# Storing rotated query and key rows as (row, head), and fetching their stacks in four transfers a quad instead of ten

## The chip, the cores and the metric

The kernel runs on one core of one Trainium2 chip. The metric is the device time of one execution in microseconds (us), smaller is better. The kernel before took 1014.62 us (median of 3 runs, 1014.4 to 1017.1).

## The reference

Two transformer-like layers run over an input `x` of 8 batches, 512 positions and 256 channels, float32:

```
xn = layernorm(x)
x  = x + attention(xn) + int8_ffn(xn)                  # layer 0
xn = layernorm(x)
x  = x + gated_comparison(xn) + receptance_ffn(xn)     # layer 1
```

Only the attention of layer 0 matters here. It has 16 heads of 64 channels:

```
q = (x @ Wq + bq).reshape(b, s, 16, 64);  k likewise;  v likewise
q, k = rope(q), rope(k)        # x0*cos - x1*sin , x0*sin + x1*cos, halves concatenated
scores = q @ k.T / 8, causal;  attn = softmax(scores);  out = (attn @ v) @ Wo + bo
```

The even channels of a head (32 of them) rotate against its odd channels (32).

## The kernel before, in words

Every float32 matrix product is split into float16 high and low parts (`wh`, `wl` for weights, `xsh`, `xsl` for the columns of x, which the page calls by these names). All of layer 0 runs in a ring of turns: `ring(n)` on each engine handles pair n of heads, 64 pairs in all (8 batches of 8 pairs), and starts at n = -5 with turns that only prepare. Four heads, two pairs, are a quad; there are 32 quads.

Queries and keys of a quad are made in two phases, f = 2*quad for the queries and f = 2*quad + 1 for the keys. A phase goes like this:

- PE, `quad_block` (L1717, matmuls at L1713): even channels of four heads into one bank, odd channels into another; 128 rows each, four heads of 32 rows.
- DVE, `even_terms` and `odd_terms` (L1378, L1392): bias from `bcol` added, multiplied with the tables `cosq`, `sinq` or `cosk`, `sink`: four products of 128x512.
- POOL, `rotate` (L616): difference and sum, `r_e` and `r_o`. ACT, `high_e` and `high_o` (L888, L896): float16 copies `hi_e`, `hi_o`. POOL, `low_e` and `low_o` (L627, L635): the remainders `lo_e`, `lo_o`.
- SP, `move_queries` or `move_keys` (L492, L506): each of these four tiles of 128x512 float16 (128 KB) is stored to DRAM (`scr`) when it is made, and read back rearranged so that the 64 channels of one head lie on the partitions: `qs` holds for each head 32 rows high even, 32 high odd, 32 low even, 32 low odd. `kd` holds the key's high parts twice (rows 0 to 63 and 64 to 127), `kz` its low parts in rows 0 to 63 and zeros under them.

`scores` (L1772) multiplies `qs` with `kd` and then with `kz` (matmuls at L1784 and L1785). The stacks exist twice, by quad parity. The first scores of a quad wait for all its loads; the loads wait for the scores of the quad before the last (`s_done`), and each load waits for the store whose data it reads (`hie_sent` and so on).

Before the change, row 32*h + r of such a tile is row r of head h. A load must therefore pick, for each of 32 partitions, four pieces of 1 KB that lie 32 KB apart in `scr`. There are four loads for a query stack and six for a key stack, 128 KB each.

What orders the work: each engine has its own list of instructions in program order, written out by hand in its `ring`, and semaphores between them. SP's list has, quad by quad, the query stores and loads, now and then stores and loads of the columns of x, then the key stores and loads. All transfers of the kernel are issued from SP.

The row order is set in three places that run once. `halves` (L396) names the source and target columns in which ACT (`act.activation`, L848, eight instructions) and DVE (`pairs_low`, L1250, instructions at L1256, sixteen) write the weights of q and k into `wh` and `wl`. The load at L463 (sixteen small transfers) lays the biases in `bcol`. `rotation_tables` (L2088) builds the tables on the host. In the preparing turns the DVE runs `pairs_low(G_Q)`, the first four rotation products, `pairs_low(G_K)`, four more products, then the weight maxima (L1215) and row statistics (L1156, L1160), and so on; ACT runs the eight weight copies and then `row_sums` (L819 to L833) of five batches.

Of the kernel before, what the change touches and what calls it, by code (L numbers as in the profile page):

```python
# [9 lines left out]
L = 64  # L10
P = 128
# [18 lines left out]
HL = L // 2  # L30
C_QK = 0
# [12 lines left out]
def build(nc, x_d, weights_d, w8_d, bqk_d, vec_d, thr_d, gate_d, tab_d, out_d):  # L44
# [11 lines left out]
    with ctx:  # L56
# [339 lines left out]
        def halves(g):  # L396

            a = g - G_Q
            for e in range(2):
                for pp in range(2):  # L400
                    src = wst_qk.rearrange("p (kq x) -> p kq x", x=8 * L)[:, :, pp * 4 * L:(pp + 1) * 4 * L]
                    src = src.rearrange("p kq (c i) -> p kq c i", i=L)[:, :, PAIR[g], e * HL:(e + 1) * HL]
                    at = (2 * a + e) * P + pp * L
                    yield src, [w[:, C_QK:C_V].rearrange("p (kq x) -> p kq x", x=8 * L)[:, :, at:at + L]
                                .rearrange("p kq (s i) -> p kq s i", s=2) for w in (wh, wl)]

        def wgroup(w, g):

# [38 lines left out]
        def _(sp):  # L447
# [12 lines left out]
            for h in range(4):  # L460
                for a, c in ((0, 1 + h % 2), (1, 3 * (h % 2))):
                    for e in range(2):
                        sp.dma_start(bcol[h * HL:(h + 1) * HL, :, a, e], b4[:, :, h // 2, c, e],  # L463
                                     allow_slow_non_contiguous=True).then_inc(b_loaded, 16)
            load_rows(3)
            load_rows(4)
# [16 lines left out]
            def fetch_columns(b):  # L483
# [5 lines left out]
                for c in range(2):  # L489
                    sp.dma_start(xs[u][c][:], xscr[b, c]).then_inc(x_in[u], 16)  # L490

            def move_queries(quad, par):  # L492

                f = 2 * quad
                after(sp, q_in[par], 64 * (quad // 2))
                for piece, tile, made_by, sent in ((0, hi_e, hie_done, hie_sent), (1, hi_o, hio_done, hio_sent),
                                                   (2, lo_e, loe_done, loe_sent), (3, lo_o, loo_done, loo_sent)):
                    sp.wait_ge(made_by, f + 1)
                    sp.dma_start(scr[par, 0, piece], tile).then_inc(sent, 16)
                after(sp, s_done, 12 * (quad - 1))  # L500
                for piece, sent in enumerate((hie_sent, hio_sent, loe_sent, loo_sent)):
                    sp.wait_ge(sent, 16 * (f + 1))
                    sp.dma_start(qs[par][piece * HL:(piece + 1) * HL],
                                 scr[par, 0, piece].rearrange("(h r) s -> r h s", h=4)).then_inc(q_in[par], 16)

            def move_keys(quad, par):  # L506

                f = 2 * quad + 1
                after(sp, k_in[par], 96 * (quad // 2))
                for piece, tile, made_by, sent in ((0, hi_e, hie_done, hie_sent), (1, hi_o, hio_done, hio_sent),  # L510
                                                   (2, lo_e, loe_done, loe_sent), (3, lo_o, loo_done, loo_sent)):
                    sp.wait_ge(made_by, f + 1)
                    sp.dma_start(scr[par, 1, piece], tile).then_inc(sent, 16)
                after(sp, s_done, 12 * (quad - 1))
                sp.wait_ge(kz_zero, 2)
                for piece, sent in enumerate((hie_sent, hio_sent, loe_sent, loo_sent)):
                    sp.wait_ge(sent, 16 * (f + 1))
                    rows = scr[par, 1, piece].rearrange("(h r) s -> r h s", h=4)
                    at = (piece % 2) * HL
                    if piece < 2:  # L520
                        sp.dma_start(kd[par][at:at + HL], rows).then_inc(k_in[par], 16)
                        sp.dma_start(kd[par][L + at:L + at + HL], rows).then_inc(k_in[par], 16)
                    else:
                        sp.dma_start(kz[par][at:at + HL], rows).then_inc(k_in[par], 16)

            def send_maxima(turn, src, count):

# [1133 lines left out]
        def _(pe):  # L1661
# [110 lines left out]
            def scores(n, h, tiles):  # L1772

                if absent(n):
                    return
                g = 2 * n + h
                par, hh = n // 2 % 2, n % 2 * 2 + h
                if h == 0 and tiles[0] == 1 and hh == 0:
                    pe.wait_ge(q_in[par], 64 * (n // 4 + 1))
                    pe.wait_ge(k_in[par], 96 * (n // 4 + 1))  # L1780
                after(pe, max_done, 4 * g - 4 + {1: 1, 0: 3, 3: 4}[tiles[0]])
                for i in tiles:
                    out, q = s_tile[i], qs[par][:, hh, i * P:(i + 1) * P]
                    pe.matmul(out, q, kd[par][:, hh, 0:(i + 1) * P], start=True, stop=False)  # L1784
                    last = pe.matmul(out, q, kz[par][:, hh, 0:(i + 1) * P], start=False, stop=True)  # L1785
                last.then_inc(s_done, 1)
# [301 lines left out]
def rotation_tables():  # L2088
# [3 lines left out]
    freq = (np.float32(1.0) / np.float32(10000.0) ** (np.float32(2.0) * np.arange(half, dtype=np.float32) / np.float32(L)))  # L2092
    ang = (np.arange(SQ, dtype=np.float32)[:, None] * freq.astype(np.float32)[None, :]).astype(np.float32)
    t = np.stack([np.cos(ang.astype(np.float64)).T, np.sin(ang.astype(np.float64)).T], axis=1).astype(np.float32)
    return np.ascontiguousarray(np.tile(t, (4, 1, 1)))


# [37 lines left out]
```

## Time and profile before

| | |
|---|---|
| median of 3 runs | 1014.62 us |
| the profiled execution, its own time | 1014.82 us |
| its span (first to last instruction) | 1012.3 us |
| PE busy | 973.6 us, 96% of the span |
| DVE / POOL / ACT busy | 840.8 / 776.1 / 744.4 us |
| packets on the one queue that carries data | 102784, 99.81 MB, 32.6% of 16 DMA engines' time |
| granted TensorE clock | 0.999 of full speed |

The span is what the trace covers; the 2.5 us between it and the execution's own time lie around it. PE busy counts overlapping matmuls once, so short waits between them can hide in it. A number such as L1784 is a line of the kernel.

### The profile page before, as it was taken

What the parts mean: (1) busy time and instruction counts of PE and PEld (TensorE: products, weight loads), DVE (VectorE), ACT (ScalarE), POOL (GpSimd) and SP (SyncE); (2) the same over time, 40 slices, a digit from 0 to 9 for tenths busy, and PEclk for the clock granted to TensorE, in tenths of its full rate; (3) what the DMA queues carried; (4) which work ended last, traced back from release to release, by engine and by line L of the source; (5) the groups of instructions that cost most, each with busy time, mean ns of one, the idle gap of its engine ahead of it and who ended that gap; (6) DMA issues with size and microseconds to landing.
All of it is one profiled execution on the core that took longest, in us unless ns stands there. A gap on an engine that the chain in (4) does not pass through costs nothing.

```text
span 1012.3 us, 23657 instructions
## 1 busy us (share of the span) xinstructions
PE 973.6 (96%) x7956; PEld 673.0 (66%) x7956; DVE 840.8 (83%) x2259; ACT 744.4 (74%) x1998; POOL 776.1 (77%) x959
## 2 busy tenths in 40 slices
PE   5889999999999999999999999999999999899998
PEld 4556665766666666666666666666666676677776
DVE  7989999788879888877787878877788778989995
ACT  5989987666676677766767676766666776889994
POOL 3777768778777787878787878787877565899995
PEclk9999999999999999999999999999999999999999
DMA  8733445243442333233333333433333200111111
GB/s 261 254 111 118 151 129 153 82 131 106 124 118 86 107 119 95 88 106 111 95 96 115 95 95 96 119 100 102 98 95 96 73 2 16 34 47 35 49 55 43
DMA packets 102902, 101.31 MB, mean 100 GB/s; under 512 B 13952, under 2 KB 98560, under 8 KB 102144
## 3 DMA queue, kind: packets, MB, share of 16 engines
q1 hardware_dynamic: 102784, 99.81, 32.6%
q8 instruction: 65, 1.06, 0.5%
q14 instruction: 53, 0.43, 0.2%
HBM read 56.25 MB, written 40.90 MB: 96 GB/s over the span
## 4 chain that ended last, share of the span: by engine, by line
PE 75%; DVE 10%; POOL 6%; ACT 4%; issue 2%; DMA 2%; SPq 0%; DVEq 0%; POOLq 0%; ACTq 0%
PE bank L1713 24%; PE bank L1810 13%; PE bank L1796 12%; PE bank L1827 8%; PE bank L1784 6%; PE bank L1785 5%; PE bank L2014 3%; PE bank L1954 3%; DVE arena L1410 2%; POOL arena L651 2%; DVE arena L1426 2%; POOL arena L714 2%; ACT arena L919 1%; DMA arena<-in_weights 1%; DVE arena L1388 1%
## 5 line engine op out<-in xcount | busy, mean ns | idle before, releaser
L651 POOL TENSOR_SCALAR arena<-arena,rc 128x128 f32<-128x128 f32 (+3 forms) x512 | 278.2, 562 | 176.5 <-DVE rc L1419 175.5
L919 ACT ACTIVATE arena<-arena,nm 128x256 f32<-128x256 f32 (+3 forms) x512 | 283.4, 554 | 109.0 <-DVE nm L1410 104.3
L1410 DVE CUSTOM_DVE_ANT_0 arena<-bank,mask_rows 128x256 f32<-128x256 f32 (+3 forms) x512 | 232.9, 483 | 88.6 <-PE bank L1785 83.4
L1796 PE MATMUL bank<-ident,arena 128*128 128x128 f32 x1280 | 211.8, 278 | 9.7 <-DVE arena L1426 4.4
L1796 PEld LDWEIGHTS bank<-ident,arena 128*128 128x128 f32 x1280 | 150.0, 141 | 68.6 <-DVE arena L1426 29.2
L1785 PE MATMUL bank<-arena 128*128 128x256 f16 (+3 forms) x512 | 152.9, 299 | 0.0
L1810 PE MATMUL bank<-arena 128*64 128x512 f32 (+3 forms) x1024 | 152.0, 439 | 0.0
L1784 PE MATMUL bank<-arena 128*128 128x256 f16 (+3 forms) x512 | 139.9, 300 | 1.5 <-DMA arena<-scr 1.5
L1810 PEld LDWEIGHTS bank<-arena 128*64 128x64 f32 x1024 | 67.8, 136 | 95.0 <-issue 70.6
L1426 DVE COPY arena<-bank 128x512 f32<-128x512 f32 (+3 forms) x256 | 124.6, 487 | 3.3 <-PE bank L1796 2.9
L927 ACT ACTIVATE arena<-bank 128x512 f32<-128x512 f32 (+3 forms) x256 | 108.6, 424 | 14.9 <-PE bank L1796 14.2
L1713 PE MATMUL bank<-xsh,wh 128*128 128x512 f16 x256 | 97.1, 379 | 3.2 <-DVE wl L1256 2.4
L1827 PE MATMUL bank<-wh,arena 128*128 128x256 f16 x512 | 99.7, 273 | 0.0
L1713 PE MATMUL bank<-xsh,wl 128*128 128x512 f16 x256 | 97.0, 379 | 0.0
L1713 PE MATMUL bank<-xsl,wh 128*128 128x512 f16 x256 | 97.0, 379 | 0.0
L919 ACT ACTIVATION_READ_ACCUMULATOR arena<-arena,nm 128x1 f32 x512 | 96.0, 187 | 0.0
L937 ACT ACTIVATE arena<-bank,bvs 128x512 f16<-128x512 f32 x64 | 44.0, 687 | 69.7 <-PE bank L1810 69.4
L1713 PE MATMUL bank<-wh,xsh 128*128 128x128 f16 x512 | 89.1, 219 | 1.9 <-DVE arena L1401 1.9
L1713 PE MATMUL bank<-wh,xsl 128*128 128x128 f16 x512 | 89.1, 219 | 0.0
L1713 PE MATMUL bank<-wl,xsh 128*128 128x128 f16 x512 | 89.1, 219 | 0.0
L623 POOL TENSOR_TENSOR arena<-arena 128x512 f32<-128x512 f32 x64 | 81.6, 1275 | 5.5 <-DVE arena L1401 5.4
L625 POOL TENSOR_TENSOR arena<-arena 128x512 f32<-128x512 f32 x64 | 83.0, 1296 | 0.0
(192 smaller groups left out, 2176.2 us busy)
## 6 DMA issues: line engine op xcount, KB each, us to landing
arena<-scr SPq DMA_DIRECT2D x320, 128.0 KB, 2.7
scr<-arena SPq DMA_DIRECT2D x256, 128.0 KB, 1.7
arena<-in_weights SPq DMA_DIRECT2D x5, 1024.0 KB, 7.8
x_sb<-in_x SPq DMA_DIRECT2D x8, 512.0 KB, 9.4
out<-x_sb SPq DMA_DIRECT2D x16, 256.0 KB, 2.2
xscr<-arena SPq DMA_DIRECT2D x12, 256.0 KB, 3.2
arena<-wh SPq DMA_DIRECT2D x40, 64.0 KB, 2.0
xsh<-xscr SPq DMA_DIRECT2D x6, 256.0 KB, 3.4
```

The costliest lines, as they stand in the source:

```text
L625: pool.tensor_tensor(r_o, t_es, t_oc, ALU.add).then_inc(r1_done, 1)
L651: last = pool.tensor_scalar(pr[slot][:, OFF[i]:OFF[i + 1]], pr[slot][:, OFF[i]:OFF[i + 1]], rc[:, slot, i:i + 1], 1.0, ALU.mult, ALU.mult)
L919: act.activation(pr[slot][:, OFF[i]:OFF[i + 1]], pr[slot][:, OFF[i]:OFF[i + 1]], ACT.Exp, scale=-1.0, bias=nm[:, slot, i:i + 1], accum_out ...
L927: act.activation(ptf[h][:, TOFF[j]:TOFF[j + 1]], (pt0, pt1)[h][:, 0:P * (NT - j)], ACT.Copy).then_inc(ptf_done[h], 1)
L1410: dve.tensor_tensor_reduce(pr[slot][:, OFF[i]:OFF[i + 1]], s_tile[i], mask_rows[:, SQ - P * (i + 1):SQ], -1.0, -MASKED, ALU.add, ALU.min, ...
L1426: dve.tensor_copy(ptf[1][:, TOFF[j]:TOFF[j + 1]], pt1[:, 0:P * (NT - j)]).then_inc(ptf_done[1], 1)
L1713: last = pe.matmul(out, lhs, rhs, start=(a == 0), stop=(a == len(pairs) - 1))
L1784: pe.matmul(out, q, kd[par][:, hh, 0:(i + 1) * P], start=True, stop=False)
L1785: last = pe.matmul(out, q, kz[par][:, hh, 0:(i + 1) * P], start=False, stop=True)
L1796: last = pe.transpose(banks[5 + h][:, (i - j) * P:(i - j + 1) * P], pr[2 * par + h][:, OFF[i] + j * P:OFF[i] + (j + 1) * P], ident[:])
L1810: last = pe.matmul(ob[h * L:(h + 1) * L, j * P:SQ], vf[:, j, h * L:(h + 1) * L], ptf[h][:, TOFF[j]:TOFF[j + 1]], start=(j == 0), stop=(j = ...
L1827: last = pe.matmul(bank[:, t * D:(t + 1) * D], o[:, slot, rows], w[:, p, :], start=(p == 0 and a == 0 and t == 0), stop=(p == NP - 1 and a ...
```

## The change

Row 4*r + h of the four tiles is now row r of head h. The weights, the biases and the tables are laid out for that order. In `scr` the four heads of one row then lie side by side, 4 KB, and pieces follow each other, so the query stack is one contiguous read of 512 KB into 128 partitions; the key stack takes three reads of 256 KB into 64 partitions each. Stores are the same. The query load now waits for all four stores; both loads of `kd` wait for both high stores, the load of `kz` for both low stores. The wait for `kz_zero` moves behind the loads of `kd`. The counts on `q_in` and `k_in` follow (64 to 16, 96 to 48).

```diff
 def halves(g):
-                    at = (2 * a + e) * P + pp * L
-                    yield src, [w[:, C_QK:C_V].rearrange("p (kq x) -> p kq x", x=8 * L)[:, :, at:at + L]
-                                .rearrange("p kq (s i) -> p kq s i", s=2) for w in (wh, wl)]
+                    at = (2 * a + e) * P
+                    yield src, [w[:, C_QK:C_V].rearrange("p (kq x) -> p kq x", x=8 * L)[:, :, at:at + P]
+                                .rearrange("p kq (i n s) -> p kq n s i", n=2, s=2)[:, :, pp] for w in (wh, wl)]
...
-                        sp.dma_start(bcol[h * HL:(h + 1) * HL, :, a, e], b4[:, :, h // 2, c, e],
+                        sp.dma_start(bcol[h:P:4, :, a, e], b4[:, :, h // 2, c, e],
...
+            def stacked(pieces):
+                return pieces.rearrange("c (r h) s -> (c r) h s", h=4)
...
 def move_queries(quad, par):
...
                 after(sp, s_done, 12 * (quad - 1))
-                for piece, sent in enumerate((hie_sent, hio_sent, loe_sent, loo_sent)):
+                for sent in (hie_sent, hio_sent, loe_sent, loo_sent):
                     sp.wait_ge(sent, 16 * (f + 1))
-                    sp.dma_start(qs[par][piece * HL:(piece + 1) * HL],
-                                 scr[par, 0, piece].rearrange("(h r) s -> r h s", h=4)).then_inc(q_in[par], 16)
+                sp.dma_start(qs[par], stacked(scr[par, 0])).then_inc(q_in[par], 16)
 def move_keys(quad, par):
...
                 after(sp, s_done, 12 * (quad - 1))
+                for sent in (hie_sent, hio_sent):
+                    sp.wait_ge(sent, 16 * (f + 1))
+                for rows in (slice(0, L), slice(L, P)):
+                    sp.dma_start(kd[par][rows], stacked(scr[par, 1, 0:2])).then_inc(k_in[par], 16)
                 sp.wait_ge(kz_zero, 2)
-                for piece, sent in enumerate((hie_sent, hio_sent, loe_sent, loo_sent)):
+                for sent in (loe_sent, loo_sent):
                     sp.wait_ge(sent, 16 * (f + 1))
-                    rows = scr[par, 1, piece].rearrange("(h r) s -> r h s", h=4)
-                    at = (piece % 2) * HL
-                    if piece < 2:
-                        sp.dma_start(kd[par][at:at + HL], rows).then_inc(k_in[par], 16)
-                        sp.dma_start(kd[par][L + at:L + at + HL], rows).then_inc(k_in[par], 16)
-                    else:
-                        sp.dma_start(kz[par][at:at + HL], rows).then_inc(k_in[par], 16)
+                sp.dma_start(kz[par][0:L], stacked(scr[par, 1, 2:4])).then_inc(k_in[par], 16)
...
 def rotation_tables():
-    return np.ascontiguousarray(np.tile(t, (4, 1, 1)))
+    return np.ascontiguousarray(np.repeat(t, 4, axis=0))
```

The target columns of the weights follow from it: in `wh` and `wl` the 32 values of one head were neighbours (2 bytes apart) and are now every fourth (8 bytes apart). The DVE reads `wh` and writes `wl` in that order too.

## Rows read from the trace of the kernel before

**Rows 1.** The page's part 4, the chain that ended last, shares by engine
```profile
PE 75%; DVE 10%; POOL 6%; ACT 4%; issue 2%; DMA 2%; SPq 0%; DVEq 0%; POOLq 0%; ACTq 0%
```
**Rows 2.** Busy time by stretch: us, PE, PEld, DVE, ACT, POOL, clock, DMA share, GB/s
```profile
63.00:200.00 137.00, 133.00 (x1049) 85.31 (x1049) 122.71 (x341) 113.14 (x309) 102.98 (x134) 1.00 0.41 123
200.00:800.00 600.00, 597.24 (x4920) 407.80 (x4919) 487.50 (x1434) 416.38 (x1172) 468.74 (x608) 1.00 0.35 105
```
**Rows 3.** Waits of PE: us in total, times, longest; the only one for a stack
```profile
PE bank L1784 <- DMA arena<-scr: 1.5, 1, 1.5
```
**Rows 4.** The chain of waits from 17 to 48 us: start, us, what
```profile
18.07 1.67 DVE wl L1256 x3
...
20.40 2.07 DVE wl L1256 x5
...
25.44 1.61 DVE wl L1256 x2
...
27.16 1.89 DVE wl L1256 x2
...
39.61 0.67 DVE arena L1401
...
47.75 0.49 ACT arena L919
```
**Rows 5.** SP's and PE's timelines in mid-ring: start, us, what
```profile
415.27 1.75 SPq L503 DMA_DIRECT2D arena<-scr  x4
423.66 3.08 SPq L513 DMA_DIRECT2D scr<-arena  x4
426.85 0.36 SPq L521 DMA_DIRECT2D arena<-scr  x1
...
428.71 0.90 SPq L524 DMA_DIRECT2D arena<-scr  x2
...
431.53 0.28 PE L1784 MATMUL bank<-arena 128*128 128x256 f16 x1
...
443.73 0.28 PE L1784 MATMUL bank<-arena 128*128 128x256 f16 x1
```
**Rows 6.** The page's part 6, DMA issues: count, KB each, median us to landing
```profile
arena<-scr SPq DMA_DIRECT2D x320, 128.0 KB, 2.7
scr<-arena SPq DMA_DIRECT2D x256, 128.0 KB, 1.7
...
xsh<-xscr SPq DMA_DIRECT2D x6, 256.0 KB, 3.4
```
**Rows 7.** SP's timeline around the first stacks
```profile
36.98 2.23 SPq L513 DMA_DIRECT2D scr<-arena  x4
...
41.15 0.30 SPq L521 DMA_DIRECT2D arena<-scr  x1
...
41.98 0.90 SPq L524 DMA_DIRECT2D arena<-scr  x2
```
**Rows 8.** Timelines of ACT, PE, DVE at the first scores; idle before in brackets
```profile
41.70 0.63 ACT L894 ACTIVATE arena<-arena 128x512 f16<-128x512 f32 x1 [0.40 <-POOL arena L623]
...
45.36 0.27 PE L1784 MATMUL bank<-arena 128*128 128x256 f16 x1 [1.48 <-DMA arena<-scr]
...
47.87 2.35 DVE L1247 SCALAR_TENSOR_TENSOR wl<-arena,inv,wh 128x2048 f16<-128x2048 f32 x1 [0.23 <-ACT wh L837]
```
**Rows 9.** Groups of instructions by shape: busy us, mean ns
```profile
L1229 DVE TENSOR_REDUCE wall<-wl 128x5 f32<-128x640 f32 x1 | 1.3, 1344 | 0.0
L1215 DVE TENSOR_REDUCE wmax<-arena 128x1 f32<-128x2048 f32 x1 | 2.3, 2276 | 0.0
L1215 DVE TENSOR_REDUCE wmax<-arena 128x1 f32<-128x512 f32 x3 | 2.0, 676 | 0.0
L874 ACT ACTIVATE w<-arena 128x512 bf16<-128x512 int32 x1 | 0.7, 652 | 0.0
L902 ACT ACTIVATE arena<-arena 128x512 f16<-128x512 f32 x64 | 39.3, 614 | 0.6 <-POOL arena L625 0.6
```

More of the change, by code:

```diff
@@ L490, in fetch_columns @@
                     sp.dma_start(xs[u][c][:], xscr[b, c]).then_inc(x_in[u], 16)
+            def stacked(pieces):
+                return pieces.rearrange("c (r h) s -> (c r) h s", h=4)
             def move_queries(quad, par):
                 f = 2 * quad
-                after(sp, q_in[par], 64 * (quad // 2))
+                after(sp, q_in[par], 16 * (quad // 2))
                 for piece, tile, made_by, sent in ((0, hi_e, hie_done, hie_sent), (1, hi_o, hio_done, hio_sent),
@@ L500, in move_queries @@
                 after(sp, s_done, 12 * (quad - 1))
-                for piece, sent in enumerate((hie_sent, hio_sent, loe_sent, loo_sent)):
+                for sent in (hie_sent, hio_sent, loe_sent, loo_sent):
                     sp.wait_ge(sent, 16 * (f + 1))
-                    sp.dma_start(qs[par][piece * HL:(piece + 1) * HL],
-                                 scr[par, 0, piece].rearrange("(h r) s -> r h s", h=4)).then_inc(q_in[par], 16)
+                sp.dma_start(qs[par], stacked(scr[par, 0])).then_inc(q_in[par], 16)
             def move_keys(quad, par):
                 f = 2 * quad + 1
-                after(sp, k_in[par], 96 * (quad // 2))
+                after(sp, k_in[par], 48 * (quad // 2))
                 for piece, tile, made_by, sent in ((0, hi_e, hie_done, hie_sent), (1, hi_o, hio_done, hio_sent),
@@ L1778, in scores @@
                 if h == 0 and tiles[0] == 1 and hh == 0:
-                    pe.wait_ge(q_in[par], 64 * (n // 4 + 1))
-                    pe.wait_ge(k_in[par], 96 * (n // 4 + 1))
+                    pe.wait_ge(q_in[par], 16 * (n // 4 + 1))
+                    pe.wait_ge(k_in[par], 48 * (n // 4 + 1))
                 after(pe, max_done, 4 * g - 4 + {1: 1, 0: 3, 3: 4}[tiles[0]])
```

## The prediction

> **What bounds the kernel now.** I read the chain of waits first. PE carries 75% of it, DVE, POOL and ACT 20% together, DMA 2% and SP's queue 0% [rows 1]. The busy times by stretch then say where PE is not full: from 200 to 800 us it is busy 597.2 of 600, from 63 to 200 us 133.0 of 137 [rows 2], so the ring is bound by PE and the whole idle time there that anything could give back is 6.8 us. Last the waits of PE: of 32 quads exactly one, the first, makes PE wait for a stack, for 1.5 us [rows 3]. The transfers that the change rebuilds are therefore hidden in 31 of 32 quads. What is left is the front: from 17 to 48 us the chain runs over DVE, where the weights' low parts (L1256) stand on it with 12 of their 16 instructions (the other four run beside PE and end just as it needs them), then over POOL and ACT [rows 4]. That is where the new row order writes with gaps.
>
> **The change, part by part.**
>
> *Ring: loads of the stacks.* Removed are 3 query and 3 key issues a quad; SP spends 1.75 us on four query loads and 426.85 to 429.61, 2.76 us, on six key loads [rows 5], about 0.44 and 0.46 an issue, so some 2.7 us of SP's time a quad go. SP is on the chain with 0% and spends its time waiting for tiles to be made; worth 0. What could hurt is that a large load lands later than four small ones, and that the query load waits for the last store. Cover: in mid-ring the query loads of a quad start at 415.27 and its key loads at 426.85, the last key issue ends at 429.61; its first score is at 443.73 [rows 5] (one turn of the ring is 443.73 - 431.53 = 12.2 us, the quad's query loads stand in turn 2 x quad - 4 and its first score in turn 2 x quad - 1). So the last key load has 14.1 us from the end of its issue, and needs about 3. A load of 128 KB lands in 2.7 us, one of 256 KB in 3.4 [rows 6]: 0.7 more for 128 KB more. A 512 KB load would then take 3.4 + 2 x 0.7 = 4.8 us and a key load 3.4, or some 4.8 for the third in a row. Cover gone would need landings of over 14 us. Cost of this part 0 in 31 quads, and I expect 0 gain too, for the same reason: nothing that PE waits for becomes earlier. Fewer and larger packets (320 loads of 128 pieces of 1 KB become 10240 pieces of 4 KB) shorten DMA time that nobody waits for.
>
> A load that starts earlier can't collide with much either: the stores are unchanged, and a query load's 512 KB are off the DMA engines long before the key stores 8.4 us later (415.27 to 423.66 [rows 5]).
>
> *First quad.* Here the key stack is late by 1.5 us as PE sees it. Before, the four key stores are issued from 36.98 to 39.21, the second one's data is only in place at 41.15, and the last load is issued by 42.88 [rows 7]; PE starts at 45.36, 2.5 us after that [rows 8]. After, the same stores come first. SP has one query issue instead of four, so the first key store can go some 0.4 us earlier (it starts at 36.98, the moment the last query issue ends), the last one can't, for it waits for POOL. Both high loads then go at 40.8 to 41.15, the low one 0.9 us later, between 41.7 and 42.4. With 3.4 us for 256 KB that is 45.1 to 45.8, and 0.4 more if it queues behind the other two: the stack lands between 45.1 and 46.2, against 45.36, so -0.3 to +0.8, most likely +0.2. What is it worth? If earlier: nothing. The chain passes over ACT (its row sums and the copy of the next weights, L919 at 47.75 [rows 4]) and not over these scores. If later: DVE must finish the four maxima of these scores before L1247, which waits 0.23 us for ACT anyway [rows 8]; so the first 0.23 us or so are free and the rest is on the path. Bounds 0 to +0.6, taken +0.1. Where the 1.5 us go: PE's next idle time is for DVE and POOL, which the same chain sets.
>
> *Weights, DVE.* Sixteen instructions of 256 elements now read `wh` and write `wl` 8 bytes apart, all on the chain. No such DVE row is in the trace, so bounds. From above: the reduction L1229 reads 640 elements 20 bytes apart in 1344 ns; packed, L1215 shows (2276 - 676)/1536 = 1.04 ns an element, so 640 packed would be 676 + 128 x 1.04 = 809, and the gaps cost 535 ns, 0.84 an element [rows 9]. 16 x 256 x 0.84 = 3.4 us. From below 0: packed elements already pass at about one per cycle in this instruction and can't become faster by gaps. The nearest row is ACT's L874, which reads int32 exactly 8 bytes apart: 652 ns against 614 for the packed copy of the same size, L902 [rows 9], that is 0.04 us for 512 elements. By that 4096 elements cost 0.3 us. I take +0.2.
>
> The Trainium skill, "SBUF — State Buffer", section "Door 1: The DMA port swizzle", says that SBUF serves lines of 16 bytes and that accesses run at full rate as long as two fall in each line. By that rule 8 bytes apart is free and 20 bytes apart is not, and the sum would have 0 here; both trace rows agree with it in kind (0.04 us, 535 ns).
>
> *Weights, ACT.* Eight copies of 512 elements with gapped writes: by L874 8 x 0.04 = 0.3 us, by the upper slope 8 x 512 x 0.84 = 3.4 us, beside the DVE ones, not on top: DVE follows ACT half by half. ACT's next wait is 0.40 us at 41.70 [rows 8], so up to 0.4 us is absorbed there, but until then its high tiles are late and with them the first stack (cover 0.23 as above). Taken +0.
>
> *Biases and tables.* Sixteen transfers of 0.5 KB to partitions 4 apart instead of 32 neighbours, the same number of pieces; the tables come whole from the host. Before, the sum over the biases starts without a wait. 0, bounds -0.1 to +0.5, from nothing better than that SP's issue of the small ones already takes longer than that of a large one.
>
> *Moved wait and merged waits.* The key loads of the first quad wait for their stores and not for POOL's zeros, which precede its first rotation; 0. The query load's wait for the last store keeps SP from nothing: behind it are the stores of the next phase, whose tiles are not yet made.
>
> Once more a rule that speaks against the change. The Trainium skill, same page and section, says that 64 partitions reach no more of the memory's ports than 32 and gives 196 GB/s for 64 of them. By that figure 256 KB pass in an estimated 1.3 us, and two of the three key loads share one half, which puts the last of them at about 45.5 in the first quad and nowhere near 14 us in the ring; no row here shows a load to 64 partitions. It would change the sum by less than 0.1 us.
>
> **Sum.** Ring 0, first stack +0.1, weights +0.2, rest 0: +0.3 us on a profiled execution of 1014.82 (span 1012.3 and 2.5 around it), which lies 0.2 above the median of the runs. On the median: 1014.62 + 0.3 = 1014.9 us.
>
> A difference below 0.3%, 3.0 us, can't be told from none here.
>
> **Rivals.**
>
> A, slower: *gapped writes are dear.* DVE pays the slope of L1229 on its sixteen weight instructions, and nearly all of them stand on the chain [rows 4]: +3.4 us, and ACT's delay adds up to 0.6 over the first stack: 1018.3 to 1018.9. It decides from 0.7 ns an element (3.0 us over 4096). For it: L1229 shows that gaps can cost. Against: there each element has its own line, at 20 bytes, and L874 at 8 bytes shows a tenth of that. Chance 0.11.
>
> B, a little faster: *the first stack does matter.* The 1.5 us wait goes in part and the front moves with it, since the chain that I read picks one releaser of several: 1014.6 - 1.5 = 1013.1. Against: the chain runs through ACT with no wait for these scores before 47.75 [rows 4]. Within 0.3%. Chance 0.15.
>
> C, faster: *the loads disturb the engines.* If engines run slower beside 1 KB pieces than beside 4 KB ones, the idle time of PE in the ring goes: at most 6.8 us, 1007.8; half of it 1011.2. For it: PE loses 4.0 us in 63 to 200 us, where DMA is at 0.41, and 2.8 in 600 us at 0.35 [rows 2]. Against: the chain in the first stretch is long on extra DVE work, none of it on a DMA. Chance 0.09.
>
> D, *it doesn't do what it says:* the single large read is spread over few DMA engines. At the mean rate in the profile, 99.81 MB in 32.6% of 16 x 1012.3 us, one engine moves 18.9 GB/s, and 768 KB on one would take 42 us, 27 too late in every quad: hundreds of us. The stores, equally contiguous in DRAM, land in 1.7 us [rows 6], so no. Chance 0.02.
>
> **How the numbers follow.** My case, no measurable change, has 0.63; with B 0.78, the chance of within 0.3%. Faster by more is C, 0.09; slower by more is A and D, 0.13. The range takes my case with both ends (0 to +3.4 for weights, 0 to +0.6 for the stack), B, and half of C: 1012.0 to 1018.3.
>
> **What would show it.** Loads of `arena<-scr` x128, with 32 of 512 KB landing in 4 to 5.5 us and 96 of 256 KB in 3 to 4.5. L1256 at 470 to 500 ns, L848 at 707 to 750. PE's wait at L1784 once, 1 to 2.3 us, L1401 of the third phase within 0.3 us of 39.61, PE busy 597 of 600 between 200 and 800. I am wrong if L1256 takes over 640 ns, if a second wait of L1784 for a DMA shows up, or if the ring between 200 and 800 moves by more than 2 us while PE's work is the same.

## The result

The kernel after takes 1021.37 us (median of 6 runs, 1018.85 to 1022.43), the kernel before in the same comparison 1014.78 us (1014.28 to 1017.1): a ratio of 1.0055, 95% interval 1.0044 to 1.0067. The medians differ by 6.6 us, and by the ratio the kernel is slower by 5.6 us (4.5 to 6.8), more in either case than the 3 us that count as a difference. The prediction was 1014.9 us, "no measurable change", with a range of 1012.0 to 1018.3. It was wrong, and the time lies above every rival but the broken transfer, D.

### The profile page after: what moved, and what is told of

The parts are those of the page before. It is cut to its first block, busy times and chain, and to the rows that moved or that the text cites. A ratio compares the mean times of both kernels' runs of the same rounds, so it can differ in the third digit from the quotient of the medians.

```text
span 1019.2 us, 23531 instructions
## 1 busy us (share of the span) xinstructions
PE 978.2 (96%) x7956; PEld 674.0 (66%) x7956; DVE 844.9 (83%) x2259; ACT 748.8 (73%) x1998; POOL 776.5 (76%) x959
## 4 chain that ended last, share of the span: by engine, by line
PE 75%; DVE 10%; ACT 5%; POOL 4%; DMA 3%; issue 2%; SPq 1%; DVEq 0%; POOLq 0%; ACTq 0%
PE bank L1714 24%; PE bank L1811 13%; PE bank L1797 12%; PE bank L1828 8%; PE bank L1785 6%; PE bank L1786 5%; PE bank L2015 3%; PE bank L1955 3%; DVE arena L1411 2%; POOL arena L652 2%; DVE arena L1427 2%; DMA scr<-arena 1%; POOL arena L715 1%; DMA arena<-in_weights 1%; ACT wh L849 1%
## 5 line engine op out<-in xcount | busy, mean ns | idle before, releaser
L1785 PE MATMUL bank<-arena 128*128 128x256 f16 (+3 forms) x512 | 140.2, 301 | 3.5 <-DMA arena<-scr 3.5
L938 ACT ACTIVATE arena<-bank,bvs 128x512 f16<-128x512 f32 x64 | 44.0, 687 | 70.2 <-PE bank L1811 70.0
```

## The profile after

The profiled execution took 1021.75 us, with a span of 1019.2 us (before 1012.3). Line numbers outside SP's list are one higher than before: L849 is L848, L1257 is L1256, L1785 is L1784. From the page: the shares of the chain by engine, then three lines of part 6 (count, KB each, median us to landing).

```profile
PE 75%; DVE 10%; ACT 5%; POOL 4%; DMA 3%; issue 2%; SPq 1%; DVEq 0%; POOLq 0%; ACTq 0%
...
scr<-arena SPq DMA_DIRECT2D x256, 128.0 KB, 1.8
arena<-scr SPq DMA_DIRECT2D x96, 256.0 KB, 4.2
arena<-scr SPq DMA_DIRECT2D x32, 512.0 KB, 3.2
```

Against [rows 1] SP's queue and the DMAs have come onto the chain. Whether the ring or the front lost is read with a marker that exists once a turn: ACT's first copy of a turn's output (L937, after L938). Timeline of ACT in the kernel before, turns 0 and 63 (start, us, what):

```profile
67.89 0.69 ACT L937 ACTIVATE arena<-bank,bvs 128x512 f16<-128x512 f32 x1 [0.46 <-PE bank L1810]
...
843.04 0.69 ACT L937 ACTIVATE arena<-bank,bvs 128x512 f16<-128x512 f32 x1 [1.72 <-PE bank L1810]
```

The same of after:

```profile
74.14 0.69 ACT L938 ACTIVATE arena<-bank,bvs 128x512 f16<-128x512 f32 x1 [0.47 <-PE bank L1811]
...
849.25 0.69 ACT L938 ACTIVATE arena<-bank,bvs 128x512 f16<-128x512 f32 x1 [1.72 <-PE bank L1811]
```

Turn 0 is late by 6.25 us, turn 63 by 6.21. In between the ring lost nothing; this difference is made ahead of turn 0. The 0.7 us that the span shows beyond it lie behind turn 63's marker, from which the traces run for another 169.3 us before and 170.0 after; the work there is the same. Busy times by stretch of after, the second stretch set 6.2 us later so that it covers the same turns (columns as in [rows 2]):

```profile
206.20:806.20 600.00, 597.26 (x4920) 407.80 (x4919) 487.40 (x1434) 416.24 (x1172) 468.70 (x608) 1.00 0.35 105
```

That is [rows 2] again. The new landing times (4.2 and 3.2 us) are in the ring, and PE doesn't notice them. Its waits, after (us in total, times, longest):

```profile
PE bank L1714 <- DVE wl L1257: 4.1, 2, 2.6
PE bank L1785 <- DMA arena<-scr: 3.5, 1, 3.5
```

Still one wait for a stack in 32 quads, but 3.5 us in place of the 1.5 of [rows 3]. The chain of the front in after, from the weight copies to the first scores (start, us, what; left out between are mainly the row sums of three batches and the query's high copies):

```profile
16.73 9.48 ACT wh L849 x8
...
40.50 0.53 ACT arena L903
...
41.04 3.81 DMA scr<-arena
...
44.92 0.51 SPq L521
...
46.19 4.71 DMA arena<-scr
...
51.04 0.27 PE bank L1785
```

Before, the chain up to 40 us was DVE's, with L1256 on it [rows 4]. Now it is ACT's: eight weight copies, then its row sums without a gap, the key's high copies, their store, the loads, and the first scores at 51.04 against 45.36 [rows 8]. The groups of the weights in the first 60 us, by shape (busy us, mean ns), before:

```profile
L848 ACT ACTIVATE wh<-arena,inv 128x512 f16<-128x512 f32 x8 | 5.0, 709 | 3.5 <-DVE inv L1241 3.5
L1256 DVE SCALAR_TENSOR_TENSOR wl<-arena,inv,wh 128x256 f16<-128x256 f32 x16 | 9.7, 676 | 0.0
```

and after:

```profile
L849 ACT ACTIVATE wh<-arena,inv 128x512 f16<-128x512 f32 x8 | 9.5, 1406 | 3.4 <-DVE inv L1242 3.4
L1257 DVE SCALAR_TENSOR_TENSOR wl<-arena,inv,wh 128x256 f16<-128x256 f32 x16 | 12.3, 944 | 0.5 <-ACT wh L849 0.5
```

ACT's copies take nearly twice as long, +4.5 us; DVE's take 2.6 us more. The eight copies are the front's common start, and they begin when the weights have landed, at 16.73 us in after (chain above) and at 17.11 before:

```profile
17.11 5.01 ACT L848 ACTIVATE wh<-arena,inv 128x512 f16<-128x512 f32 x8 [3.52 <-DVE inv L1241]
```

Counted from there, turn 0 is late by 6.6 us and not by 6.25. Then SP's timeline of after (columns as in [rows 7]):

```profile
3.17 11.88 SPq L463 DMA_DIRECT2D bcol<-in_bqk  x16
...
39.33 0.32 SPq L507 DMA_DIRECT2D arena<-scr  x1
40.52 2.68 SPq L516 DMA_DIRECT2D scr<-arena  x4
```

The sixteen bias loads, issued in 10.65 us before, take 11.88.

## The experiments

Theories after the result. G: the gapped weight writes delay the front. S: SP and the DMA queue do, by the biases' slower issue and the first stack's large loads. K: TensorE's granted clock, which falls in the front of after behind PE's 3.5 us wait (0.61 of full speed in 52 to 56 us, so in part at the lower of its two levels, 1.2 GHz; before 1.00, 2.4 GHz), costs the rest. Beside each time stands the *shift*: the start of turn 0's marker against 67.89 us. It comes from one profiled execution of each kernel, in which ACT's first weight copy begins anywhere from 15.96 to 17.20 us, as the first weights land. The *shift from the copy*, in brackets, leaves that scatter out: it counts both times from that copy.

**The weights alone, and all the rest without them.** `e2_gapped_only` is the kernel before with the weights' new target columns (the first hunk of the diff); `e1_packed_writes` is the kernel after with the old ones (shown is e1's edit; that of e2 is its reverse):

```diff
-                    at = (2 * a + e) * P
-                    yield src, [w[...][:, :, at:at + P].rearrange("p kq (i n s) -> p kq n s i", n=2, s=2)[:, :, pp] for w in (wh, wl)]
+                    at = (2 * a + e) * P + pp * L
+                    yield src, [w[...][:, :, at:at + L].rearrange("p kq (s i) -> p kq s i", s=2) for w in (wh, wl)]
```

> The kernel before with one thing added: the weights are written 8 bytes apart as in the changed kernel (and so in an order that its loads do not expect). Loads, stores, biases and tables are those of before. W: 1019.5 to 1021.5 us, the ring late by 5 to 6.3 us. L: 1014.8 to 1016.5 us.

> The changed kernel with one thing undone: the weights of q and k are written packed, as before, so their columns are no longer in the order that the rest uses. Theory W (the loss is the gapped writes of the weights: ACT's eight copies take 1402 ns instead of 707, start to start +0.57 us each, 4.5 us on the chain, and the rest follows from that): 1014 to 1016 us, L849 back at 707 ns. Theory L (the loss is in the loads: the first key stack lands later, 4.7 us for its last load instead of 2.9, PE idles 3.5 us before its first scores, and TensorE's clock drops): 1018 to 1021 us, PE still idle some 3 us before the first scores with the clock low behind it.

Measured: e2 1019.64 us, ratio 1.0042 [1.0028, 1.0056], shift 5.50 (5.9). e1 1018.99 us, 1.0036 [1.0024, 1.0049], shift 4.72 (5.1), with PE's wait for the first stack at 4.8 us. The kernel before had a median of 1014.94 in this comparison, so the halves of the change cost 4.7 and 4.1 us alone (4.3 and 3.7 by the ratios), and 6.6 together (5.6): they overlap. Neither G nor S alone is the cause.

**The weights written packed in the new order.** `e3_host_order` is the kernel after with the columns of Wq and Wk laid out in the new order ahead of time, so that ACT and DVE write neighbours; it computes the same.

```diff
-                    src = src.rearrange("p kq (c i) -> p kq c i", i=L)[:, :, PAIR[g], e * HL:(e + 1) * HL]
+                    at = (2 * a + e) * P + pp * L
+                    src = wst_qk.rearrange("p (kq x) -> p kq x", x=8 * L)[:, :, at:at + L].rearrange("p kq (s i) -> p kq s i", s=2)
...
+    wqk = row_head(a["L0_attn_Wq"], a["L0_attn_Wk"])   # (row, head) columns
```

> The changed kernel with the columns of Wq and Wk put into (quad, q or k, even or odd, row, head) order by the host, so that the copies on ACT and DVE read and write packed. W: as e1, 1013.5 to 1016 us, the first kernel that has the few loads without the loss. L: 1018 to 1021 us. The reductions over the staged weights read contiguously here; they took 1214 ns for 1024 elements before and should stay.

Measured: 1018.59 us, 1.0035 [1.0023, 1.0046], shift 3.87 (3.8). In time like e1: some 3 us of the 6.6 are won back, and 3.7 stay (1018.59 against 1014.94), that have nothing to do with the gapped weights. The shifts of e1 and e3 from the copy are 1.3 us apart, though ACT's and DVE's weight instructions take the same in both (5.0 and 9.7 to 9.8 us) and loads and biases are alike. A difference of that size between two single traces therefore means little by itself; below, the times stand beside it.

**What a gap costs.** `p1_steps` is the kernel before with another step in each piece of the q and k weights, which changes the order of those columns:

```diff
+                    high, low = {(0, 0): ((packed, packed), (step2, step2)), (0, 1): ((step4, step4), (step4, step4)),
+                                 (1, 0): ((step4, packed), (step4, packed)), (1, 1): ((packed, step4), (packed, step4))}[a, e][pp]
```

> The kernel before, with a different step in each of the weight pieces, to measure durations (its weights are out of order). ACT in order: packed; 4 bytes apart; 8 apart; 8 apart with the two neighbouring heads innermost; 8 apart twice; packed twice. DVE in pairs of instructions: packed; 4 apart read and written; 8 apart read and written, twice; 8 apart read, packed written, twice; packed read, 8 apart written, twice. Theory S16 (a 16-byte line is served at full rate as long as two accesses fall in it): all like packed, ACT 707, DVE 473 ns; refuted already by 1402 and 775 in the changed kernel. Theory G (any gap between float16 writes costs, for two neighbours are otherwise joined): 4 bytes apart as dear as 8, reads on DVE 473 to 500, writes 775. Theory B8 (one access for 8 bytes): 4 apart stays at 707 and 473, 8 apart 1402 and 775, whether read or written.

Of ACT's eight copies in it the first four (start, us, what) are: packed; 4 bytes apart; 8 bytes apart; the same places with the two neighbouring heads innermost, so that two adjacent values are written one after the other:

```profile
16.91 0.72 ACT L861 ACTIVATE wh<-arena,inv 128x512 f16<-128x512 f32 x1 [3.48 <-DVE inv L1254]
17.54 0.85 ACT L861 ACTIVATE wh<-arena,inv 128x512 f16<-128x512 f32 x1
18.25 1.43 ACT L861 ACTIVATE wh<-arena,inv 128x512 f16<-128x512 f32 x1
19.42 0.79 ACT L861 ACTIVATE wh<-arena,inv 128x512 f16<-128x512 f32 x1
```

DVE's in the same kernel, where 29.25 reads `wh` 8 bytes apart and writes packed, and 29.65 reads packed and writes 8 bytes apart:

```profile
20.20 0.50 DVE L1269 SCALAR_TENSOR_TENSOR wl<-arena,inv,wh 128x256 f16<-128x256 f32 x1
20.60 0.80 DVE L1269 SCALAR_TENSOR_TENSOR wl<-arena,inv,wh 128x256 f16<-128x256 f32 x1
...
29.25 0.47 DVE L1269 SCALAR_TENSOR_TENSOR wl<-arena,inv,wh 128x256 f16<-128x256 f32 x1
29.65 0.78 DVE L1269 SCALAR_TENSOR_TENSOR wl<-arena,inv,wh 128x256 f16<-128x256 f32 x1
```

(20.20 is 4 bytes apart, 20.60 8 bytes in both.) DVE's reading is free (0.47), the writing is dear (0.78), and of the steps tried only the one by which a single 2-byte value falls into 8 bytes: two of them, 4 bytes apart or written in turn, cost ACT 0.07 to 0.13 us on 512 elements against 0.7. No run has ACT read 2-byte values with gaps.

**Which engine's writes.** By the instruction prices ACT loses 4.5 us and DVE 2.6; e2 doesn't tell which one delays the front. Two kernels from the one before, with only one of the two targets gapped:

```diff
-                    yield src, [... for w in (wh, wl)]
+                    yield src, [packed(wh), gapped(wl)]      # s3_gapped_dve_only
+                    yield src, [gapped(wh), packed(wl)]      # s4_gapped_act_only
```

> The kernel before, where only VectorE's half of each weight piece (the low parts) is written eight bytes apart; ScalarE writes its half packed. The two halves then disagree in their order, so the product is not that of the reference. Theory A (ScalarE's writes carry the loss): VectorE's sixteen take 0.77 in place of 0.47 us beside ScalarE's, first turn late by 0 to 1.0 us, 1014.7 to 1015.9. Theory B (VectorE's writes carry at least half): first turn late by 2.5 us or more, 1017 or more.

> The counterpart: only ScalarE's half of each weight piece (the high parts) is written eight bytes apart, VectorE writes its half packed; the product is not that of the reference. Theory A: ScalarE's eight take 1.40 in place of 0.71 us, first turn late by 4 to 5.5 us, 1018.7 to 1020. Theory B: late by 2.5 us or less, 1017.3 or less.

Measured: s3 1019.86 us, 1.0046 [1.0033, 1.0059], shift 4.08 (4.6); s4 1019.38 us, 1.0042 [1.003, 1.0055], shift 4.21 (4.7). Both theories missed on one of the two: each engine alone carries nearly all of it. In s3 the chain of the front is DVE's, in s4 ACT's. Chain of s3:

```profile
19.39 4.03 DVE wl L1258 x6
...
28.41 6.27 DVE wl L1258 x6
...
41.59 0.75 DVE arena L1390
```

DVE's sixteen take 14.3 us there (1070 ns each, for ACT's packed halves come early and more of the sixteen fall beside POOL, at 1.14 to 1.73 us). Chain of s4:

```profile
16.64 9.50 ACT wh L850 x8
...
40.45 2.87 DMA scr<-arena
...
45.66 3.04 DMA arena<-scr
48.84 0.37 PE bank L1786
```

The front thus has two chains of about one length, DVE's through the weights and rotations and ACT's through the weights, row sums and the key's copies. Counted from the copy, all of what is added arrives: of ACT's 4.5 us 4.7, of DVE's 4.6 us 4.6. Neither chain had a cover that shows here. Either one delayed is enough, and sparing one of them wins back only 1.2 to 1.3 us of e2's 5.9.

Not all of e2's delay is the writes themselves. Three blocks of six matmuls stand on its chain, and each takes 0.8 to 1.0 us longer than before. Chain of e2:

```profile
23.82 2.45 PE bank L1713 x6
...
32.17 2.29 PE bank L1713 x6
34.46 2.24 PE bank L1713 x6
```

Chain of the kernel before, the second of its three such blocks (the others take 1.48 and 1.47):

```profile
29.18 1.46 PE bank L1713 x6
```

Busy times of e2, the columns as in [rows 2]:

```profile
22.00:26.00 4.00, 3.63 (x11) 1.14 (x10) 2.94 (x6) 4.00 (x5) 0.00 (x0) 0.57 1.09 360
32.00:36.00 4.00, 3.83 (x10) 1.22 (x11) 3.73 (x7) 3.94 (x16) 0.79 (x1) 0.58 0.08 34
```

The granted clock is 0.57 and 0.58 there, and 1.00 before. Ahead of these stretches PE had waited 1.94 and 2.56 us for the gapped `wl`, where it waits 0.51 and 1.85 before. So 2.6 us of the chain of e2 are time at the low clock, behind PE's longer waits for the slow writes. In after the clock falls at the second of these places too (0.67 in 32 to 36 us), but the chain there is ACT's, and in s4, where nearly the same is lost, it stays at 1.00 in this stretch. What e2 would take with the clock held up was not tested.

**The rest of the loss: biases or loads.** Four variants of e3 (weights packed). `g1_bias_rows` lays each bias piece on 32 neighbouring partitions again, which attaches the biases to other rows. `g3_split_queries` and `g2_split_both` fetch the query stack, or both stacks, in four and six loads as before, each contiguous in DRAM; `g4_split_one_bias` is g2 with the biases laid out ahead of time and one transfer:

```diff
-                        sp.dma_start(bcol[h:P:4, :, a, e], ...              # e3
+                        sp.dma_start(bcol[h * HL:(h + 1) * HL, :, a, e], ...  # g1
+                    sp.dma_start(qs[par][piece * HL:(piece + 1) * HL], stacked(scr[par, 0, piece:piece + 1]))   # g3, g2
+                        sp.dma_start(t, stacked(scr[par, 1, piece:piece + 1]))                                # g2
+            sp.dma_start(bcol[:], bqk_d).then_inc(b_loaded, 16)             # g4
```

> The kernel e3_host_order (weights ordered by the host, loads as in the change, +3.7 us over before) with the sixteen bias transfers writing 32 neighbouring partitions again, as before the change (so the biases meet the wrong rows). Theory B (the stepped bias transfers hold SP's queue 1.3 us longer, 11.96 instead of 10.65, the loads of x start 1.3 us later and the DMA engines are full up to 36 us when the first query stores go, which land late): 1015 to 1016.5 us, the first query load at 36.5 to 37 instead of 38.1. Theory M (merged loads: one query load waits for the last store and holds up SP and the first key store behind it; three key loads of 256 KB land 4.6 us after issue instead of 2.9): 1017.5 to 1018.6 us.

> e3_host_order with only the query loads split by piece. If SP's wait for the last query store is the larger half of M: the first key store is issued near 37.3 instead of 38.5, but the last key store is bound by POOL (made at 38.9), so the first scores move from 48.65 to 47.5 to 48.3, and the time to 1017.5 to 1018.5 us. If the key loads' landing is the larger half: no change, 1018.6.

> e3_host_order with the loads split by piece as before the change, four for queries and six for keys, each behind its own store, but each reading 32 rows of 4 KB in one contiguous piece. Output as the reference. M: 1014.5 to 1016 us, first scores at 45 to 46.5 us, the clock stays up. B: 1017 to 1018.5 us.

> g2_split_both with the biases laid out by the host and fetched in one transfer, so that SP issues the loads of x some 10 us earlier. Output as the reference. B and M agree: at least as fast as g2, 1013 to 1015.5 us, stores of the first phases landing in 1.7 to 2.5 us. If early loads of x get in the way of the weights, the maxima at L1268 end later than 14.5 us and it is slower than g2.

Measured: g1 1016.37, 1.0007 [0.9998, 1.0016], shift 1.09 (1.3). g3 1018.72, 1.0029 [1.0018, 1.004], shift 2.40 (3.4). g2 1017.65, 1.0020 [1.0011, 1.0029], shift 2.32 (2.7). g4 1015.62, 1.0001 [0.9992, 1.0011], shift -0.41 (0.0), PE's wait 1.5 as before. Counted from the copy, taking the bias steps away from e3 brings 2.4 us (2.8 by the ratios), splitting both loads 1.1 (1.5 by the ratios, whose intervals overlap). With both gone the kernel before is back, and not beaten.

**The same from the other end.** `r4_before_stepped_bias` is the kernel before with only the bias transfers stepped (`bcol[h:P:4]`), `r3_change_bias_rows` the kernel after with only those on neighbouring partitions; both attach biases to the wrong rows. `g5_merged_one_bias` is e3 with one bias transfer and merged loads.

```diff
-                        sp.dma_start(bcol[h * HL:(h + 1) * HL, :, a, e], ...
+                        sp.dma_start(bcol[h:P:4, :, a, e], ...   # r4; r3 is the reverse, on the kernel after
```

> The kernel before with only the sixteen bias transfers stepped over partitions 4 apart (wrong rows again). Theory B: SP's queue 1.3 to 1.6 us later from 15 us on, query stores landing late behind the loads of x, keys late by about 1.3 us: 1016 to 1017.5 us. If the split loads absorb it: 1015.2.

> The changed kernel with the bias transfers to 32 neighbouring partitions again (biases meet the wrong rows), weights still written 8 bytes apart, loads merged. If the parts added up: 1021.4 - 2.3 = 1019.1. If ACT's 4.5 us shift the stores past the time at which the DMA engines are full, the bias delay is hidden behind it and nothing changes: 1020.5 to 1021.4.

> e3_host_order with the biases in one transfer, loads merged as in the change: the change with both side effects removed. Output as the reference. Before + 0 to +1.5: g1 says that with merged loads and no step in the biases 1.2 us are left, which come from the loads (first scores at 45.9) and the clock behind them. If early loads of x empty the DMA engines sooner, stores and loads land faster and it reaches 1015 (as g4 did with split loads); 1015 to 1016.5.

Measured: r4 1017.21, 1.0019 [1.001, 1.0027], shift 2.75 (3.1). r3 1021.76, 1.0063 [1.005, 1.0075], shift 6.7 (6.9), no less than the 6.25 (6.6) of after. g5 1017.03, 1.0010 [1.0, 1.002], shift 2.23 (2.6). SP's timeline of r4:

```profile
3.18 11.65 SPq L463 DMA_DIRECT2D bcol<-in_bqk  x16
14.87 1.14 SPq L451 DMA_DIRECT2D x_sb<-in_x  x2
```

and the chain of r4 at the first stacks:

```profile
30.89 4.74 DMA scr<-arena
...
37.44 4.56 DMA scr<-arena
...
44.35 3.04 DMA arena<-scr
```

One microsecond more of issue (11.65 against 10.65) moves the loads of x, 512 KB each, from 13.86 to 14.87. Busy time by stretch of before, then of r4 (us, PE, PEld, DVE, ACT, POOL, clock, DMA share, GB/s):

```profile
32.00:34.00 2.00, 1.89 (x10) 0.66 (x9) 1.83 (x4) 1.94 (x11) 1.74 (x3) 1.00 0.91 344
34.00:36.00 2.00, 1.28 (x7) 0.43 (x6) 2.00 (x2) 1.97 (x11) 2.00 (x2) 1.00 0.30 103
```

```profile
32.00:34.00 2.00, 1.88 (x9) 0.70 (x8) 2.00 (x3) 1.94 (x10) 1.72 (x3) 1.00 1.00 397
34.00:36.00 2.00, 1.28 (x16) 0.57 (x14) 2.00 (x3) 1.91 (x9) 2.00 (x2) 1.00 0.61 214
```

The input still fills the DMA engines when the first query stores come. The first of them lands 4.74 us after its issue at 30.89 in r4, and 3.96 us before. With the biases in one transfer (g4, g5) the loads of x start 10 us earlier, the last lands by 26.6 us, and the same store takes 1.72 us: this crowding is shown. One microsecond at 3 us is 0.4 us at the first query load (35.64 against 35.20), 2.2 at the first scores (47.52 against 45.36) and 2.75 at turn 0's marker.

Most of that growth comes with the key stores: the first takes 4.56 us, before 2.71, and all six loads behind it wait. Whether the query loads are what it meets is not shown. DMA packets by queue and kind in 38 to 41 us (packets, MB, share of 16 engines), before:

```profile
q8 instruction: 1, 0.02, 2.3%
```

and in r4:

```profile
q8 instruction: 1, 0.02, 4.0%
```

One packet of 16 KB that carries instructions passes there, for 1.1 us before and 1.9 in r4, while the share of all engines from 40 to 41 us is 0.05 in r4 and the key stores land only at 42.0. That they stood behind this packet on its engine is a rival that no kernel tests. It would make part of the 2.75 us a chance of timing.

In r3 the neighbouring bias rows bring nothing, since the gapped weights delay the first query stores to 35.40 anyway.

**The clock.** `r1_fill` is e3 with more of the idle matmuls that keep PE busy ahead of the first scores, which hold the granted clock up:

```diff
-                    fill(30)
+                    fill(80)
```

> e3_host_order (+3.7 us over before) with 80 instead of 30 filler matmuls on PE ahead of the first scores (3.1 us more at 62 ns each), so that PE idles some 1.5 us there instead of 4.65. Theory K (the low clock behind that idle time costs: scores and even channels took 4.23 us at a granted clock of 0.62 in 48 to 52 us, against 2.38 at 1.00 in the kernel before): 1.0 to 1.9 us faster, 1016.7 to 1017.6, clock 1.00 in 48 to 52. Rival (the chain is set by DMA and ACT, the slow matmuls only fill time that is lost anyway): 1018.6.

Measured: 1019.07, 1.0039 [1.0026, 1.0053], shift 4.1 (4.4) against e3's 3.9 (3.8). Busy times of e3 and of r1 from 50 us:

```profile
50.00:54.00 4.00, 4.00 (x31) 2.29 (x30) 3.92 (x7) 4.00 (x15) 2.79 (x2) 0.70 0.68 226
```

```profile
50.00:54.00 4.00, 4.00 (x53) 3.26 (x52) 4.00 (x4) 4.00 (x15) 3.20 (x2) 1.00 0.67 227
```

The clock is back at 1.00 and PE does 53 matmuls instead of 31 in 4 us, and nothing is won: K falls for the stretch behind the first scores. For the low clock at 22 to 36 us in e2 it was not tested, since e3's front has none there. In r1 the chain goes through DVE's L1248 instead (3.33 us, in e3 2.84, beside POOL's remainders).

**The ring, with the front spared.** `s1_ring_merged_late` is g4, where only the first two quads are fetched load by load and the other thirty in the merged form of the change; it computes the same. `s2_one_bias_alone` is the kernel before with the biases in one transfer.

```diff
+                if quad >= 2:
+                    sp.dma_start(qs[par], stacked(scr[par, 0])).then_inc(q_in[par], 16)   # s1; kd and kz likewise
```

> This is the variant with host-ordered weights and one bias transfer, with the loads of the first two quads one by one and those of the other thirty merged as in the change. My theory (the merged loads cost time only before the first scores; in the ring they have cover): same as the variant with all loads one by one, 1015.0 to 1015.9 us, first ring turn within 0.5 us of the kernel before (67.9 us). Rival (the change gains in the ring once the front is spared, by fewer packets in the queue): below 1014.5. Rival (the merged loads cost in the ring too, a little each quad): 1016.5 or more, with the first turn in place and the last turn late.

> The kernel before with its bias columns laid out ahead of time and loaded by one transfer in place of sixteen. My theory (issue time of the sixteen bias transfers on SP sets when the input and so the first stacks come): SP reaches the input loads some 9 us earlier, but the weights set the first scores, so at most 0.5 us is won: 1014.3 to 1014.9. Rival (SP's bias issues are on the path in the kernel before already): 1012 to 1013.5. Rival (the earlier input loads take the DMA engines from the weights): 1015.5 or more.

Measured: s1 1014.55, 0.9998 [0.999, 1.0007], shift -0.62 (0.0). s2 1015.29, 1.0006 [0.9997, 1.0015], shift -0.68 (0.5), although its loads of x start 10 us earlier. In thirty of 32 quads the merged loads are free and gain nothing. Nothing tried beats the kernel before.

## Why the prediction was wrong

| what is changed against the kernel before | shift, us | from the copy, us | kernel |
|---|---|---|---|
| ACT's weight writes gapped | 4.2 | 4.7 | s4 |
| DVE's weight writes gapped | 4.1 | 4.6 | s3 |
| both | 5.5 | 5.9 | e2 |
| biases to every fourth partition | 2.75 | 3.1 | r4 |
| merged loads, neighbouring bias rows | 1.1 | 1.3 | g1 |
| merged loads, one bias transfer | 2.2 | 2.6 | g5 |
| split loads, one bias transfer | -0.4 | 0.0 | g4 |
| biases and merged loads | 3.9 to 4.7 | 3.8 to 5.1 | e3, e1 |
| all, the change | 6.25 | 6.6 | after |

*What bounds it, and the ring:* right. 31 quads cost nothing, one wait for a stack remained, and the ring took its 597.3 of 600 us. The landing of 256 KB was put at 3.4 us from another transfer and was 4.2; 512 KB at 4.8 and was 3.2. Neither mattered there.

*Weights, ACT: "Taken +0".* The step that failed most. It had a top end of 3.4 us, said to lie "beside the DVE ones, not on top"; measured 4.5 us, and alone (s4) all of it arrives. That the two lie side by side was right: 4.7 and 4.6 alone, 5.9 together. Two errors in it. The price came from L874, which *reads* 8 bytes apart; the change writes, and p1 shows a read at 0.00 (DVE) and a write at 0.3 (DVE, 256 elements) to 0.7 us (ACT, 512). And a cover of 0.4 us [rows 8] had been found, against a top end of 3.4: some 3 us of it had to arrive by the prediction's own numbers. The upper end should have been carried through ACT's chain.

*Weights, DVE: "I take +0.2".* Its range of 0 to 3.4 held the 2.6 of after, though not the 4.6 of s3; the choice "nearest row" failed for the same reason, a read for a write. Its sign of being wrong is there: L1256 was not to pass 640 ns and took 944 in the mean. "All on the chain" and the 12 of 16 read before it don't agree either. Rival A, with 0.11, had this mechanism and almost this price (1018.3 to 1018.9, where 3.4 to 4.0 on 1014.62 give 1018.0 to 1018.6), but left ACT at 0.6; e2 took 1019.64.

The rule cited from the Trainium skill, "SBUF — State Buffer", section "Door 1: The DMA port swizzle", two accesses for each line of 16 bytes at full rate, made 8 bytes apart free. For reads the trace agrees (0.47 us in p1); for 2-byte writes it does not (1.43 us against 0.72), and the measurement decides: two values to 8 bytes are nearly free there, one is not.

*Biases and tables: "0, bounds -0.1 to +0.5".* Failed. Sixteen issues took 1.2 us longer in after (11.88 against 10.65; over all kernels 11.19 to 11.96 against 10.22 to 10.65), which I had covered by "before, the sum over the biases starts without a wait": I asked who waits for the biases, not what is queued behind them on SP. Alone it is worth 2.75 us of shift (1.9 us of time by r4's ratio); in the change it hides under the weights.

*First quad: "taken +0.1", bounds 0 to +0.6.* Mis-sized. The last key load went out at 46.19 and took 4.71 us, where 3.4 and at most 0.4 more had been allowed. From the landing of the key's second high store to that of the last load 6.1 us pass (44.85 to 50.91), before 4.1 (41.14 to 45.23), and these 2 us are what PE waits longer. The Trainium skill's rule on 64 partitions ("SBUF — State Buffer", section "Door 1: The DMA port swizzle"), put there at "less than 0.1 us", may bear on it: 256 KB into 64 partitions land in 4.2 us and 512 KB into 128 in 3.2, so bytes don't set the time and partitions may. But the three key loads are in flight together, the query load is not, and the 256 KB loads of x's columns, into 128 partitions, went from 3.4 to 4.5 us in the same kernel; no run separates the two. The step "keeps SP from nothing", on the merged wait, held in after: SP stood until 39.33, when the last query store was in, but the first key store, at 40.52, waited for ACT. It failed in e3 and e1, where the wait for late query stores holds SP until 38.11 and 36.98 and puts the key stores on the chain. The 512 KB then lie ahead of these stores. The second took 3.81 us in after and 4.27 in g5, but 3.68 before as well; in g4, with split loads and one bias transfer, it took 1.72. Merged loads cost between 1.1 us of shift (g1; 1.3 from the copy) and 2.6 (g5 against g4); why these two differ stays open, and two single traces can lie that far apart.

*Sum.* The terms don't add up: 5.5 + 2.75 + 1.1 = 9.4 us against 6.25 (from the copy 10.3 against 6.6), since two chains and a queue lead to the same scores and each hides part of the others. *C and B:* no gain in the ring, none from a shorter wait for the first stack (s2 has 1.0 us, and is no faster).

## What to carry to other kernels

Price a layout change by the side it writes: a strided read that costs nothing in the trace says nothing of a strided write. Where two engines prepare the same thing side by side, find the slack of each against the other before one is called cover, and test one at a time; here neither had any that shows. Count such slack from an event that both traces share, for the landing of the first load alone moved these fronts by up to 1.2 us. For an edit of a small transfer at the start, ask what is queued behind it on the issuing engine, and whether the large transfers that it delays will meet the first stores.

## What the runs showed of the hardware

- ACT writes 2-byte values 8 bytes apart at half speed (512 elements: 1.43 against 0.72 us), DVE at about 0.6 (256 elements: 0.78 against 0.47). 4 bytes apart they take 0.85 and 0.50; the 8-byte places written two neighbours at a time 0.79 on ACT. DVE's reads of 2-byte values 8 bytes apart are free (0.47).
- A transfer from SP whose 32 target partitions are 4 apart takes longer to issue than one to 32 neighbours: sixteen took 11.19 to 11.96 us (seven kernels) against 10.22 to 10.65 (seven), with the same pieces and bytes.
- A contiguous read from DRAM of 256 KB into 64 partitions, three of them in flight, lands in 4.2 us (median), one of 512 KB into 128 in 3.2, one of 128 KB into 32 in 2.7 (g2).
- A 128 KB store landed in 1.7 us with the DMA engines little used (g4, g5), and in 3.96 (before) to 4.74 us (r4) behind the input's loads. A 16 KB packet that carries instructions took 1.1 us before and 1.9 in r4 at 38 to 41 us.
- PE's granted clock stayed at 1.00 over waits of 0.51 and 1.85 us in the front of the kernel before, and was 0.57 and 0.58 behind waits of 1.94 and 2.56 us in e2; six matmuls of L1713 then took 2.24 to 2.45 us in place of 1.46 to 1.48.
- DVE's weight instruction (256 elements, two inputs) takes 0.47 us alone and 1.49 beside POOL's rotation, gapped 0.77 and 1.73. The same instruction over 2048 elements takes 2.35 us where it starts ahead of POOL's remainder, which then takes 2.32 in place of 1.16 (before, e2). It takes 3.19 where the remainder began 0.1 us ahead of it (after) and 2.84 where it began 0.5 us ahead (e3).
